# A graph network layer on one core: five groups of edges moved from the dense to the scattered way

## The chip, the core and the metric

The kernel runs on one core of one Trainium2 chip. The metric is the device time of the program in microseconds (us), as the median of several runs. Engines are named as the profile names them: PE is TensorE, ACT ScalarE, DVE VectorE, POOL GpSimd, SP the engine that here only issues transfers.

## The reference, cut to what matters

There are 6250 nodes with 64 features and 200000 edges; the edges are sorted by `dst`, and `src` is random. Each edge's message goes through a small network, the messages are averaged over the edges of the same `src`, and a second network works on the nodes.

```python
h = jnp.maximum(_layernorm(x, axis=-1), 0.0)
row, col = (edge_index[0], edge_index[1])          # row = src, col = dst
msg = jnp.concatenate([h[col], edge_attr], axis=1)
msg = jnp.maximum(msg @ W1a + b1a, 0.0) @ W1b + b1b
summed = jax.ops.segment_sum(msg, row, num_segments=x.shape[0])
counts = jax.ops.segment_sum(jnp.ones((row.shape[0],), msg.dtype), row, num_segments=x.shape[0])
agg = summed / jnp.maximum(counts, 1.0)[:, None]
out = jnp.maximum(jnp.concatenate([h, agg], axis=1) @ W2a + b2a, 0.0) @ W2b + b2b
return x + out
```

## The kernel before

**Tiling.** The edges are cut into 261 groups of 768 (six tiles of 128, `TPG = 6`). For a group, PE first makes the hidden rows: three f32 matmuls of the edge features and six bf16 matmuls that add the rows of the node table (`z`, L1207 and L1212); ACT applies Relu into `r3` (L684, the split). W1b is applied after the averaging, so what is summed over `src` are these hidden rows. There are two ways to sum them, and the constants `DENSE` and `SPARSE` say how many groups go each way.

**The dense way** (140 groups) stays on the chip. PE takes off the bf16 parts to get exact remainders (`take_off`, L1219), routes the rows into ten buckets with one-hot matrices (`route`, 30 matmuls of 196 columns, L1243), ACT copies the buckets out in ten pieces (`keep_routed`, L701). When five groups (`MACRO = 5`, a macro) are in the buckets, PE sums each bucket over its nodes (`sum_nodes`, 150 small matmuls per group, L1257), and DVE makes the one-hots (L937, L952) and adds the sums to `dense` (L959).

**The scattered way** (121 groups) goes through memory. PE adds rows with equal `src` inside a tile (`combine`, 18 matmuls, L1231), ACT copies the result to a slot of `vv` (`keep_rows`, L689), DVE computes which row is to be added where (`pick_first`, L924 and L929), and POOL issues six indirect adding transfers of 128 rows (`scatter`, L524). They go in turn to three tables in memory, `sums0` to `sums2`, and a table takes its next transfer only when its last one has landed. `vv` has four slots (`SR = 4`).

**Order.** All engines walk the same list of cycles, which is what sets the order of all work around the change. A cycle routes one dense group, sums two buckets of the macro before it, and handles no or one scattered group:

```python
for t, n in enumerate(FIRST + BODY + LAST):
    cycle(s, n, Count(t), t < DENSE, t >= MACRO)
```

`n` is the number of scattered groups of cycle `t`. The first five cycles (`FIRST`) have no sums yet, and have `u` matmuls (L1266) in their place; the last five (`LAST`) have sums alone. Between them lie `DENSE - MACRO` = 135 cycles (`BODY`), over which 114 scattered groups are spread as evenly as whole numbers allow: the body cycles without one are numbers 0, 6, 12, 19, 25, 32 and so on, 21 in all. Each engine takes its part of a cycle in its own written order, and waits on semaphores for the others. A scattered group's waits are these:

```python
pool.wait_ge(sidx_ready, done(g.value(1)))             # scatter, POOL
pool.wait_ge(rows_ready, done(g.value(1)))
pool.wait_ge(scattered[t], before.times(16, 16))       # before each of the six
act.wait_ge(comb_ready, done(g.value(1)))              # keep_rows, ACT
act.wait_ge(groups_ended, done(g.value(1 - SR)))
pe.wait_ge(rows_ready, done(g.value(-1)))              # combine, PE
```

So ACT writes group `g` into `vv` only when POOL has issued group `g - 4`; behind that wait stand ACT's other copies of the cycle.

**Ends.** Ahead of the loop the node table is made, and DVE ranks all edges of the dense groups in their buckets with arrays of `DT = (DENSE + 1) * 6` columns (L848 to L889, L873). After the last scatter SP reads the three tables back, POOL adds a bias (L614) and zeroes padding (L618), and a last loop of 13 turns works on the nodes (L1089 to L1129 on DVE, L1318 to L1338 on PE).

Of the kernel before, what the change touches and what calls it, by code (L numbers as in the profile page):

```python
# [47 lines left out]
FIRST_POWER = (127 + 60) * POWER_STEP  # L48
SHIFT = 1.5 * 2.0 ** 23

MACROS = 28
DENSE = MACROS * MACRO
SPARSE = 121
FIRST = (1, 1, 1, 1, 1)
LAST = (1, 0, 1, 0, 0)
EVEN = SPARSE - sum(FIRST) - sum(LAST)
BODY = tuple((t + 1) * EVEN // (DENSE - MACRO) - t * EVEN // (DENSE - MACRO) for t in range(DENSE - MACRO))
DG = DENSE + 1
# [67 lines left out]
def cycles(cycle):  # L126


    s = Count(0)
    for t, n in enumerate(FIRST + BODY + LAST):  # L130
        cycle(s, n, Count(t), t < DENSE, t >= MACRO)
# [3 lines left out]
def gnn_kernel(nc, x, e_t, src_col, dst_col, src_row, dst_row, weights, row_biases, out):  # L135
    f32, i32, i16, bf16 = mybir.dt.float32, mybir.dt.int32, mybir.dt.int16, mybir.dt.bfloat16
    ALU, ACT, AX = mybir.AluOpType, mybir.ActivationFunctionType, mybir.AxisListType
    assert DENSE + SPARSE == GROUPS and GROUPS + 2 <= ALL and DG * TPG <= COLS and 2 * D == P and N_NODES < REAL
    assert N_NODES % NT == 0 and ROWP * ROWG % SIDES == 0 and max(*FIRST, *BODY, *LAST) == 1

    with ExitStack() as ctx:
# [195 lines left out]
        with nc.Block() as block:  # L337

            @block.sync
            def _(sp):  # L340
# [91 lines left out]

                for kind, last in ((S, SPARSE - sum(LAST) + SR + 1), (DN, DENSE + DR + 1)):
                    for s in range(RING[kind]):
# [34 lines left out]
            def _(pool):  # L469
# [83 lines left out]
                with pool.If(fit == 1):  # L553
# [5 lines left out]
                    for t in range(TABLES):  # L559
                        pool.wait_ge(scattered[t], 16 * (1 + len(range(t, SPARSE * TPG, TABLES))))  # L560
                with pool.Else():
# [4 lines left out]
                    def fetch(kind, g):  # L566
                        pool.wait_ge(gidx_ready[kind], done(g.value(1)))
                        pool.sem_inc(pool_past, 1)
                        gather(2 if kind == DN else g.mod(2))
                        if kind == DN:  # L570
                            pool.wait_ge(slots_ready, done(g.value()))
                            pool.dma_start(dsrc, ids[0:1, bass.ds(g.times(GE), GE)].to_broadcast([P, GE])).then_inc(dsrc_in, 16)
# [9 lines left out]
                    def cycle(s, n, t, routes, sums_too):  # L582
                        ended = Count(s.base + min(t.base, DENSE), s.per + t.per, t.turn)
                        for k in range(1, n + 1):
                            if s.per or s.base + k < SPARSE:
                                fetch(S, s.plus(k))
# [40 lines left out]
            def _(act):  # L627
# [48 lines left out]
                def main(fit):  # L676
                    def split(kind, g, r):

                        if r == 0 and not fit:
                            act.wait_ge(zsum_ready[kind], done(g.times(3, 3)))  # L680
                        else:
                            act.wait_ge(z_ready[kind], done(g.times(READS[kind], r + 1)))
                        z = z_ps[kind][:, 0:TPG * D].rearrange("p (t d) -> p t d", d=D)
                        nc.scalar.activation(r3[kind][:, :, PARTS[r]:PARTS[r] + D], z, ACT.Relu).then_inc(split_ready[kind], 1)  # L684

                    def keep_rows(g):
                        act.wait_ge(comb_ready, done(g.value(1)))
                        act.wait_ge(groups_ended, done(g.value(1 - SR)))
                        nc.scalar.activation(vv[:, g.mod(SR), :, :],  # L689
                                             c_ps[g.mod(2)][:, 0:TPG * R].rearrange("p (t w) -> p t w", w=R),  # L690
                                             ACT.Copy).then_inc(rows_ready, 1)
# [28 lines left out]
                    def cycle(s, n, t, routes, sums_too):  # L720
                        if n:
                            keep_rows(s)
                        if n and (s.per or s.base + 1 < SPARSE):
                            split(S, s.plus(1), 0)
# [654 lines left out]
```

## Time and profile before

| | us |
|---|---|
| median of 3 runs | 1632.61 (1630.75 to 1633.25) |
| the profiled execution | 1626.88 |
| its span, first to last instruction | 1625.0 |
| PE busy | 1478.5 (91%) |
| DVE busy | 1416.8 (87%) |
| POOL busy | 1205.2 (74%) |
| ACT busy | 1047.7 (64%) |

The busy times are of one profiled execution, whose own time is 1.88 us over its span and 5.73 us (0.35%) under the median. On POOL only the instruction that issues a transfer counts as busy. It does not count the waits, nor the issue overhead between two of them. Times in the trace are counted from the first instruction.

### The profile page before, as it was taken

What the parts mean: (1) busy time and instruction counts of PE and PEld (TensorE: products, weight loads), DVE (VectorE), ACT (ScalarE), POOL (GpSimd) and SP (SyncE); (2) the same over time, 40 slices, a digit from 0 to 9 for tenths busy, and PEclk for the clock granted to TensorE, in tenths of its full rate; (3) what the DMA queues carried; (4) which work ended last, traced back from release to release, by engine and by line L of the source; (5) the groups of instructions that cost most, each with busy time, mean ns of one, the idle gap of its engine ahead of it and who ended that gap; (6) DMA issues with size and microseconds to landing.
All of it is one profiled execution on the core that took longest, in us unless ns stands there. A gap on an engine that the chain in (4) does not pass through costs nothing.

```text
span 1625.0 us, 77131 instructions
## 1 busy us (share of the span) xinstructions
PE 1478.5 (91%) x31132; PEld 1400.4 (86%) x31132; DVE 1416.8 (87%) x4789; ACT 1047.7 (64%) x2192; POOL 1205.2 (74%) x794
## 2 busy tenths in 40 slices
PE   4378999999999999999999999999999999999946
PEld 3257999999999999999999999999999999899934
DVE  7857988989989899988898988988889989889947
ACT  5167766666666767666666667766666767666503
POOL 5166777788778788777787788787777878777771
PEclk9689999999999999999999999999999999999977
DMA  5666776767767677666677766776767767667651
GB/s 174 239 118 99 122 106 107 122 107 108 120 105 118 111 113 119 105 115 109 105 123 106 118 108 109 122 109 107 115 110 118 113 105 125 104 113 109 95 118 58
DMA packets 279402, 187.16 MB, mean 115 GB/s; under 512 B 190543, under 2 KB 275404, under 8 KB 278281
## 3 DMA queue, kind: packets, MB, share of 16 engines
q1 hardware_dynamic: 174070, 152.93, 39.5%
q0 software_dynamic: 104976, 29.30, 27.7%
q8 instruction: 246, 4.03, 1.0%
q14 instruction: 110, 0.90, 0.2%
HBM read 147.94 MB, written 34.17 MB: 112 GB/s over the span
## 4 chain that ended last, share of the span: by engine, by line
PE 73%; ACT 11%; issue 5%; DMA 5%; DVE 3%; POOL 2%; DVEq 0%; SPq 0%; POOLq 0%; ACTq 0%
PE l_ps L1257 31%; PE l_ps L1243 22%; PE z_ps L1207 8%; ACT area L701 7%; PE z_ps L1219 5%; PE c_ps L1231 5%; DMA sums<-vv,sidx 3%; ACT r_d L684 3%; PE z_ps L1212 2%; POOL sums L524 1%; DMA area<-sums 1%; DMA xs<-in_x 1%; DVE rank L873 1%; ACT r_s L684 0%; DVE area L857 0%
## 5 line engine op out<-in xcount | busy, mean ns | idle before, releaser
L524 POOL DMA_INDIRECT sums<-vv,sidx x726 | 1157.5, 1594 | 359.6 <-issue 169.7
L1257 PE MATMUL l_ps<-area 128*128 128x64 bf16 (+1 forms) x21000 | 793.0, 193 | 1.0 <-issue 0.4
L701 ACT ACTIVATE area<-l_ps 64x392 bf16<-64x392 f32 x1400 | 688.1, 491 | 127.4 <-PE l_ps L1243 97.1
L1257 PEld LDWEIGHTS l_ps<-area 128*128 128x128 bf16 x21000 | 746.0, 98 | 22.8 <-issue 1.9
L1243 PE MATMUL l_ps<-r_d,oh 128*128 128x196 bf16 x4200 | 483.6, 250 | 16.0 <-issue 8.3
L952 DVE TENSOR_SCALAR area<-iota,local 128x640 bf16<-128x640 int16 x1400 | 475.4, 404 | 4.9
L1243 PEld LDWEIGHTS l_ps<-r_d,oh 128*128 128x128 bf16 x4200 | 334.5, 96 | 26.9 <-ACT area L701 12.2
L684 ACT ACTIVATE r_d<-z_ps 128x384 f32<-128x384 f32 x423 | 207.8, 491 | 196.5 <-PE z_ps L1219 182.2
L937 DVE TENSOR_SCALAR oh<-iota,rank 128x640 bf16<-128x640 int16 x846 | 281.7, 401 | 0.0
L959 DVE TENSOR_TENSOR dense<-l_ps,dense 128x325 f32<-128x325 f32 x280 | 137.8, 492 | 115.2 <-PE l_ps L1257 110.0
L917 DVE TENSOR_TENSOR r_s<-r_s 128x384 f32<-128x384 f32 x242 | 134.3, 555 | 4.1
L1219 PE MATMUL z_ps<-r_d,minus_b 128*128 128x384 bf16 x282 | 96.1, 341 | 44.5 <-ACT r_d L684 28.4
L906 DVE TENSOR_SCALAR same<-ids_s,srcf 128x128 bf16<-128x128 int16 x726 | 131.2, 269 | 0.0
L689 ACT ACTIVATE vv<-c_ps 128x396 f32<-128x396 f32 x121 | 60.5, 500 | 94.2 <-PE c_ps L1231 93.7
L1207 PE MATMUL z_ps<-wts,et_d 128*128 128x128 f32 x846 | 121.1, 280 | 0.0
L1207 PE MATMUL z_ps<-wts,et_s 128*128 128x128 f32 x726 | 112.5, 292 | 2.4 <-issue 2.4
L1207 PEld LDWEIGHTS z_ps<-wts,et_d 128*128 128x128 f32 x846 | 105.8, 192 | 0.0
L684 ACT ACTIVATE r_s<-z_ps 128x384 f32<-128x384 f32 x121 | 59.1, 488 | 71.0 <-PE z_ps L1212 69.1
L1231 PE MATMUL c_ps<-r_s,same 128*128 128x64 bf16 (+1 forms) x2178 | 93.1, 193 | 2.0 <-issue 1.8
L1207 PEld LDWEIGHTS z_ps<-wts,et_s 128*128 128x128 f32 x726 | 92.3, 195 | 2.6 <-issue 2.5
L899 DVE TENSOR_SCALAR hots_d<-ids_d,basew 128x384 bf16<-128x384 int16 x284 | 84.3, 337 | 0.0
L1231 PEld LDWEIGHTS c_ps<-r_s,same 128*128 128x128 bf16 x2178 | 78.1, 97 | 6.4 <-issue 2.4
(133 smaller groups left out, 737.0 us busy)
## 6 DMA issues: line engine op xcount, KB each, us to landing
ids_s<-ids SPq DMA_DIRECT2D x248, 192.0 KB
et_d<-in_e_t SPq DMA_DIRECT2D x143, 192.0 KB
ids_d<-ids SPq DMA_DIRECT2D x143, 192.0 KB
et_s<-in_e_t SPq DMA_DIRECT2D x124, 192.0 KB
sums<-vv,sidx POOLq DMA_INDIRECT x726
sums<-dense POOLq DMA_DIRECT2D x3, 1657.5 KB
wp_d<-p_table SPq DMA_DIRECT2D x286, 15.8 KB
wp_s<-p_table SPq DMA_DIRECT2D x248, 15.8 KB
```

Source lines behind the costliest of these rows:

```text
L524: nc.gpsimd.indirect_dma_start(out=sums[t][:, :], out_offset=bass.IndirectOffsetOnAxis(ap=index, axis=0), in_=rows, in_offset=None, comput ...
L684: nc.scalar.activation(r3[kind][:, :, PARTS[r]:PARTS[r] + D], z, ACT.Relu).then_inc(split_ready[kind], 1)
L701: ins = nc.scalar.activation(routed[on, t.div(MACRO).mod(2), first:second + 1:second - first, t.mod(MACRO), :], bank[on, :, :], ACT.Copy)
L917: nc.vector.tensor_tensor(r3[S][:, :, PARTS[r + 1]:PARTS[r + 1] + D], r3[S][:, :, at:at + D], halves(S)[:, :, at:at + D], ALU.subtract).th ...
L937: ins = nc.vector.tensor_scalar(oh1[:, k, :], iota[:], pos[:, bass.ds(t.value(k * DG), 1)], None, ALU.is_equal)
L952: nc.vector.tensor_scalar(oh2[:, g, :], iota[:], local[:, n.mod(2), g:g + 1], None, ALU.is_equal).then_inc(nodes_ready, 1)
L959: nc.vector.tensor_tensor(part, l2_ps[h][:, 0:BW], part, ALU.add).then_inc(summed, 1)
L1207: nc.tensor.matmul(z_ps[kind][:, j * P:(j + 1) * P], et[kind][:, slot, j * P:(j + 1) * P], wts[:, C_W1A_BOT:C_W1A_BOT + P], start=j == 0, ...
L1219: nc.tensor.matmul(z_ps[kind][:, 0:TPG * D], minus_b[:], halves(kind)[:, :, PARTS[r]:PARTS[r] + D], start=False, stop=True, skip_group_che ...
L1231: t = nc.tensor.matmul(c_ps[b][:, k * R:k * R + n], same[:, b, k, :], halves(S)[:, k, PARTS[r]:PARTS[r] + n], start=r == 0, stop=r == 2)
L1243: ins = nc.tensor.matmul(l1_ps[f % 2][:, i * RW:(i + 1) * RW], oh1[:, k, block * P:(block + 1) * P], halves(DN)[:, k, :], start=k == side ...
L1257: ins = nc.tensor.matmul(l2_ps[h][:, u * W:u * W + w], oh2[:, g, u * P:(u + 1) * P], rows[:, PARTS[r]:PARTS[r] + w], start=g % MACRO == 0 ...
```

## The change

Three constants change. One macro less goes the dense way: 27 macros, 135 groups. The scattered groups become 126. The last cycle gets a scattered group, so there are five in the first five cycles, 118 over the 130 of the body and three in the last five. The number of groups stays 261, and the order within a cycle stays as it is. The body has twelve cycles without a scattered group, numbers 0, 10, 21, 32, 43 and so on.

```diff
-MACROS = 28
+MACROS = 27
 DENSE = MACROS * MACRO
-SPARSE = 121
+SPARSE = 126
 FIRST = (1, 1, 1, 1, 1)
-LAST = (1, 0, 1, 0, 0)
+LAST = (1, 0, 1, 0, 1)
```

In the body on ACT, the first place where the two orders differ is the end of cycle 11, body number 6. In these rows `vv` is the copy of a scattered group, `r_s` the Relu of the next one, `area` the ten bucket copies of a dense group and `r_d` its three splits. Before:

```order
L689 ACTIVATE vv<-c_ps 128x396
L684 ACTIVATE r_s<-z_ps 128x6x64
L701 ACTIVATE area<-l_ps 64x2x196 x10
L684 ACTIVATE r_d<-z_ps 128x6x64 x3
L701 ACTIVATE area<-l_ps 64x2x196 x10
L684 ACTIVATE r_d<-z_ps 128x6x64 x3
L689 ACTIVATE vv<-c_ps 128x396
```

And now, in the same cycles:

```order
L689 ACTIVATE vv<-c_ps 128x396
L684 ACTIVATE r_s<-z_ps 128x6x64
L701 ACTIVATE area<-l_ps 64x2x196 x10
L684 ACTIVATE r_d<-z_ps 128x6x64 x3
L689 ACTIVATE vv<-c_ps 128x396
L684 ACTIVATE r_s<-z_ps 128x6x64
L701 ACTIVATE area<-l_ps 64x2x196 x10
```

The cycle without `vv` and `r_s` is gone from here; the next one comes four cycles later, and such cycles are eleven apart instead of six or seven.

At the end of the main loop on ACT, the rows begin with the last cycle of the body. Before:

```order
L689 ACTIVATE vv<-c_ps 128x396
L684 ACTIVATE r_s<-z_ps 128x6x64
L701 ACTIVATE area<-l_ps 64x2x196 x10
L684 ACTIVATE r_d<-z_ps 128x6x64 x3
L689 ACTIVATE vv<-c_ps 128x396
L684 ACTIVATE r_s<-z_ps 128x6x64
L689 ACTIVATE vv<-c_ps 128x396
```

And now:

```order
L689 ACTIVATE vv<-c_ps 128x396
L684 ACTIVATE r_s<-z_ps 128x6x64
L701 ACTIVATE area<-l_ps 64x2x196 x10
L684 ACTIVATE r_d<-z_ps 128x6x64 x3
L689 ACTIVATE vv<-c_ps 128x396
L684 ACTIVATE r_s<-z_ps 128x6x64
L689 ACTIVATE vv<-c_ps 128x396
L684 ACTIVATE r_s<-z_ps 128x6x64
L689 ACTIVATE vv<-c_ps 128x396
```

Two scattered groups followed the body's last, and now three do.

## Rows read from the trace of the kernel before

**Rows 1.** The page: span, busy time, share, instructions; then groups of part 5.

```profile
span 1625.0 us, 77131 instructions
PE 1478.5 (91%) x31132; PEld 1400.4 (86%) x31132; DVE 1416.8 (87%) x4789; ACT 1047.7 (64%) x2192; POOL 1205.2 (74%) x794
...
L524 POOL DMA_INDIRECT sums<-vv,sidx x726 | 1157.5, 1594 | 359.6 <-issue 169.7
```

**Rows 2.** Busy time of each engine in four stretches, clock, DMA share, GB/s.

```profile
core 0: us, PE busy (x) PEld busy (x) DVE busy (x) ACT busy (x) POOL busy (x), PEclk, DMA share, GB/s
141.80:1532.50 1390.70, 1344.94 (x29638) 1294.81 (x29639) 1257.49 (x4340) 958.86 (x1985) 1086.90 (x682) 1.00 0.71 112
1532.50:1559.40 26.90, 25.75 (x775) 24.21 (x772) 21.64 (x66) 0.99 (x2) 22.63 (x15) 1.00 0.38 29
1559.40:1565.80 6.40, 0.00 (x0) 0.00 (x0) 0.50 (x1) 0.00 (x0) 5.45 (x4) 0.76 0.31 19
1565.80:1625.00 59.20, 28.94 (x130) 20.12 (x130) 37.56 (x104) 14.60 (x39) 17.91 (x17) 0.67 0.34 113
```

**Rows 3.** The scatters of L524 alone, in two stretches: POOL busy and count.

```profile
154.60:1508.70 1354.10, 1062.60 (x666) 1.00 0.71 112
1508.70:1565.80 57.10, 47.55 (x30) 0.97 0.51 64
```

**Rows 4.** What POOL waited for, 154.6 to 1508.7: us, times, longest.

```profile
POOL sums L524 <- issue: 156.6, 481, 2.4
POOL sums L524 <- DMA sums<-vv,sidx: 104.4, 173, 2.4
POOL sums L524 <- DVE sidx L929: 36.4, 12, 6.9
```

**Rows 5.** Instructions of POOL in order of time: start, us, idle before.

```profile
88.63 1.68 POOL L524 DMA_INDIRECT sums<-vv,sidx  x1 [40.05 <-DVE sidx L929]
...
154.67 1.55 POOL L524 DMA_INDIRECT sums<-vv,sidx  x1 [6.94 <-DVE sidx L929]
...
1472.41 1.56 POOL L524 DMA_INDIRECT sums<-vv,sidx  x1 [2.85 <-DVE sidx L929]
...
1508.78 1.55 POOL L524 DMA_INDIRECT sums<-vv,sidx  x1 [1.05 <-DMA sums<-vv,sidx]
...
1564.22 1.55 POOL L524 DMA_INDIRECT sums<-vv,sidx  x1 [0.30 <-issue]
1570.47 7.18 POOL L614 TENSOR_TENSOR xs<-xs,rowb 128x3328 f32<-128x3328 f32 x1 [4.70 <-issue]
```

**Rows 6.** Instructions of PE in order of time, at cycle borders.

```profile
141.86 0.70 PE L1243 MATMUL l_ps<-r_d,oh 128*128 128x196 bf16 x6 [0.57 <-ACT ht L717]
...
181.94 0.72 PE L1231 MATMUL c_ps<-r_s,same 128*128 128x66 bf16 x18
...
192.51 0.71 PE L1231 MATMUL c_ps<-r_s,same 128*128 128x66 bf16 x18
...
211.97 0.71 PE L1231 MATMUL c_ps<-r_s,same 128*128 128x66 bf16 x18
...
1532.57 10.31 PE L1257 MATMUL l_ps<-area 128*128 128x65 bf16 x300
```

**Rows 7.** What ACT's copy to `vv` waited for, whole span.

```profile
ACT vv L689 <- PE c_ps L1231: 93.7, 79, 10.2
```

**Rows 8.** The chain that ended last, near its end: start, us.

```profile
1564.22 3.28 DMA sums<-vv,sidx
1567.65 2.66 issue
1570.57 0.35 SPq L445
...
1603.14 0.41 PE l_ps L1318 x2
...
1614.29 0.66 PE l_ps L1318 x2
```

**Rows 9.** Groups by shape: busy, mean ns; ranking of the dense edges.

```profile
L873 DVE COPY_PREDICATED rank<-area,l_ps 128x423 f32<-128x423 uint16 x20 | 11.4, 622 | 1.1 <-PE l_ps L1183 0.2
L857 DVE TENSOR_SCALAR area<-area 128x846 bf16<-128x846 f32 x10 | 5.2, 591 | 0.0
```

**Rows 10.** Busy time in the second half of the first cycles.

```profile
120.00:142.00 22.00, 15.76 (x167) 13.12 (x166) 12.88 (x48) 16.91 (x35) 17.38 (x11) 0.95 0.69 111
```

## The prediction

> **What bounds the kernel now.** I read the busy times first, and they point to PE: 91% of the span, and 1344.94 of 1390.70 us in the body of the main loop, from the first routing matmul at 141.86 to the last cycle's end at 1532.57 [rows 1, 2, 6]. By the same rows POOL looks free, with 74% of the span. A change that takes work from PE and gives it to POOL then looks like a clear gain. The second view to read is POOL's waits, because its busy time leaves out what stands between two scatters. From 154.67, where the first group of the body starts, to 1508.78 POOL issued 666 scatters, 111 groups, in 1354.1 us, 12.20 us each [rows 3, 5]. In that time it waited for DVE's indices, that is for work, 36.4 us, and 6.94 of them lie before the first scatter of the stretch [rows 4, 5]. So it was short of work for only 29.5 us. The rest of its idle time is the overhead of issue and waits for an earlier scatter to land, and these come with every group. **A scattered group costs POOL (1354.1 - 29.5) / 111 = 11.93 us**, of which 1062.60 / 111 = 9.57 are busy [rows 3]. POOL is thus occupied for 98% of the stretch (1324.6 / 1354.1). The third view is the end: PE has nothing after 1559.4, while POOL issues until 1565.77, its last transfer lands at 1567.5, and only then does the final stage begin [rows 2, 5, 8]. So two engines bound the kernel, nearly equally, and POOL is the one that ends last.
>
> **PE's side of a cycle.** Matmuls of `combine` start at 181.94 and 192.51, one cycle with a scattered group apart: 10.57 us. The next starts at 211.97, after one with and one without: 19.46, so a cycle without costs 19.46 - 10.57 = 8.9 [rows 6]. I take 9.0, since over the body 1390.7 = 114 x T + 21 x 9.0 then gives T = 10.54, which fits the 10.57. With these two costs the 29.5 us come out again: between two empty cycles (6.43 cycles apart, 5.43 groups) PE takes 5.43 x 10.54 + 9.0 = 66.2 us and POOL 5.43 x 11.93 = 64.8, so POOL idles 1.4 us in each of 21 stretches, 29 us in all. That agreement is why I trust 11.93 as a cost that does not depend on how short of work POOL is.
>
> **What the change takes from PE.** The body becomes 118 cycles of 10.54 and 12 of 9.0, 1351.7 us, or 39.0 less. On average PE then offers a scattered group every 1351.7 / 118 = 11.46 us. Of the work in the cycles nothing else changes; DVE (1257.49 of 1390.70 busy in the body, [rows 2]) and ACT lose with the five dense groups more than five scattered ones give them.
>
> **What it gives to POOL.** POOL needs 11.93 us where PE offers one each 11.46. Now an empty cycle comes after 9.83 groups, for which PE takes 9.83 x 10.54 + 9.0 = 112.6 us and POOL 117.3. POOL falls 4.7 us further behind in each of these twelve stretches and is never short of work after its first body group; the 29.5 us vanish, and that is all the slack there is. Its own waits before that point stay: the first scatter comes at 88.63, and body number 0 is empty in both kernels, so the 6.94 us stay [rows 5]. When POOL is three groups behind (3 x 11.93 = 36 us, after some eight of the twelve stretches), the four slots of `vv` are full: ACT waits for POOL before L689, behind it stand ACT's bucket copies, and PE waits for those. That stall costs nothing more, since POOL has three groups in hand then; it only takes back the time PE had won. Before, no such wait shows but one: the longest of ACT before L689 is 10.2 us, and all 93.7 us are put down to PE [rows 7].
>
> **The sum.** From 154.67 POOL had 116 groups to do and has 121 now. In the last stretch, where few loads run beside it, five groups took 57.1 us, 11.42 each, at a DMA share of 0.51 against 0.71 [rows 3]. I count seven groups of that kind now: POOL is up to four behind when the body ends, and three follow. So 114 x 11.93 + 7 x 11.42 = 1360.0 + 79.9 = 1439.9 us, against 1565.8 - 154.67 = 1411.1 before: **+28.8 us**. The ranking ahead of the loop works on 816 columns instead of 846, 3.5% of some 20 us of DVE work on that chain (11.4 and 5.2 are its two largest groups, [rows 9]): -0.7. The final stage of 59.2 us waits for POOL alone and stays [rows 2, 8]. PE will have been idle longer when it begins, but it begins at the lower of its two levels already: the granted clock over the stage is 0.67 [rows 2], and its transposes take 0.66 us a pair against 0.41 at the higher one [rows 8]. I bound a shift of the clock's rise at 2 us either way and take 0. The third group in the last five cycles adds 0.7 us of `combine` to PE [rows 6] and one copy to ACT; both hide under POOL's backlog, and without that they would cost 1 to 2 us. All together +28.1. On the profiled execution that is 1626.9 + 28.1 = 1655.0 with a span of 1653; on the median of the runs shown, 5.7 above it, **1632.6 + 28 = 1661**.
>
> **How sure the 11.93 is.** Everything hangs on it: 0.1 us is 11 us in the time. Below, the nearest row is the 11.42 of the last stretch; above, the three groups from 1472.41 to 1508.78 took 12.12 each [rows 3, 5]. Each bound is an end, over 114 groups: -58 us and +22 us. I keep the middle value because the body's loads per time hardly change. A dense group's features and ids come at each 10.4 us instead of each 10.3, and the scattered groups' loads come a little closer in the time before the slots are full.
>
> The SBUF page of the Trainium skill (SBUF — State Buffer, section "SBUF: two separate sides") says that some DVE operations lock a port pair that GpSimd needs, and that GpSimd then cannot write the descriptors of its transfers. By that rule a less busy DVE would make scatters shorter. The trace leaves little for it: a scatter took 1.595 us on average in the body (1062.60 / 666) and 1.585 in the last stretch [rows 3], so even if all of this were gained, it would be 6 x 0.01 x 114 = 7 us, and the change leaves DVE nearly as busy.
>
> **The rivals.** (1) **POOL keeps up and PE is the bound.** If landings become quicker, because fewer dense loads compete, and a group falls to 11.46 us or less, POOL follows PE. Then the body ends at 141.9 + 1351.7 = 1493.6, POOL issues its last 33.2 us later as now (1565.77 - 1532.57) and 11.4 more for the third group: 1538.2. That is 27.6 us earlier, a time of 1605. For it: 11.42 was seen, at a DMA share of 0.51. Against it: a group needs 9.57 us of issue alone, the overhead is at each scatter, and the share in the body will stay near 0.7, since loads follow cycles. The DMA page of the skill (DMA: Bandwidth & Descriptors, section "SWDGE vs HWDGE vs iDMA") says that each DMA engine takes turns between the queues of the two kinds of transfer, which would make a landing depend on the loads beside it; the two rows agree in direction. (2) **A cheaper scatter, but not enough.** Between 11.6 and 11.75 us a group the gain and the loss meet: no change lies at 11.93 - 28 / 114 = 11.68. This decides from 0.25 us less waiting, half of what a group waits now beyond the overhead of about 0.3 us at each of six scatters (11.93 - 9.57 - 1.8 = 0.56). (3) **Scatters collide more.** With ten scattered groups in a row instead of five or six, 12.12 us may be the rule: +22 more, 1683. (4) **The stall at full slots costs PE its clock.** With ACT waiting, PE could fall to its lower level and cycles grow beyond POOL's pace, so that POOL starves again. In the first cycles PE was busy 15.76 of 22 us, less than it would be here, and was still granted 0.95 [rows 10]. So I take it as small: 10 us or so on top, 1671, within the range. That the change does not do what it says is not in question: the constants alone set the cycles.
>
> **How the numbers follow.** POOL-bound near 11.93, 1645 to 1677: 0.77. More collisions or a clock loss beyond that: 0.09. The middle case, about 1632 to 1645: 0.07, of which 0.03 within 0.2% and 0.04 above it. PE-bound or near it, under 1629: 0.07. Two tenths of a percent, 3.3 us, is about what a measurement of this kernel can tell from no change. Faster is 0.07, same 0.03, slower 0.77 + 0.09 + 0.04 = 0.90. The range of 1640 to 1679 leaves out the PE-bound case, a part of the middle one and the far end of the collisions, some 0.16.
>
> **What would show it.** In the profile after: scatters x756; POOL waiting for DVE's indices under 55 us in the whole span, of which 40.05, 6.94 and a little lie before 155; 11.9 us a group in the body; the last scatter at about 1594; PE's matmuls ending some 40 us or more before it, where it was 6.4; ACT waiting several times, for over 1 us, before L689 late in the body; PE busy about 40 us less. It would be wrong if a group cost under 11.7 us, and then POOL's waits for landings would be the row that moved; or if POOL still waited for indices every eleven cycles.

## The result and the profile after

| | before | after |
|---|---|---|
| median of 6 runs each, us | 1632.89 (1626.44 to 1633.79) | 1640.05 (1638.41 to 1647.67) |
| ratio, 95% interval | | 1.0077 [1.0053, 1.01] |
| the profiled execution, its span | 1626.88, 1625.0 | 1639.26, 1637.5 |

The changed kernel is 7.2 us slower by the medians, and 12.4 us by the two profiled executions. Forecast were 28 us. The direction held and the size did not.

The page of the changed kernel answers [rows 1]: span, busy time, and the group of the scatters.

```profile
span 1637.5 us, 75449 instructions
PE 1449.8 (89%) x30312; PEld 1371.8 (84%) x30312; DVE 1399.0 (85%) x4739; ACT 1017.2 (62%) x2137; POOL 1253.6 (77%) x824
...
L524 POOL DMA_INDIRECT sums<-vv,sidx x756 | 1206.0, 1595 | 325.2 <-issue 179.3 <-DMA sums<-vv,sidx 97.4 <-DVE sidx L929 47.9
```

PE lost 28.7 us of busy time and the kernel got slower. The scatters are 756 as they must be, and one still takes 1595 ns of POOL (1594 before). What shrank is the idle time before them: 325.2 us for 756, where 359.6 stood before 726.

The stretches of [rows 3] again, the scatters of L524 alone, with the borders moved to the start of the last six groups: 115 groups of the body, then those six. Columns: window, length, POOL busy and count, clock, DMA share, GB/s.

```profile
153.60:1511.00 1357.40, 1101.42 (x690) 0.99 0.70 113
1511.00:1580.00 69.00, 57.15 (x36) 0.86 0.42 46
```

And instructions of POOL, the counterpart of [rows 5]: start, us, idle before.

```profile
153.69 1.56 POOL L524 DMA_INDIRECT sums<-vv,sidx  x1 [8.38 <-DVE sidx L929]
...
1578.03 1.55 POOL L524 DMA_INDIRECT sums<-vv,sidx  x1 [0.31 <-issue]
1584.05 7.18 POOL L614 TENSOR_TENSOR xs<-xs,rowb 128x3328 f32<-128x3328 f32 x1 [4.47 <-issue]
```

A group took 1357.4 / 115 = 11.80 us in the body. The last six took 68.6 / 6 = 11.43 each, and all 121 took 1579.58 - 153.69 = 1425.9 us, 11.78 each. The forecast had 11.93 in the body.

The waits over the whole span, the counterpart of [rows 4, 7]: us in total, times, longest.

```profile
POOL sums L524 <- DMA sums<-vv,sidx: 97.4, 186, 2.3
POOL sums L524 <- DVE sidx L929: 47.9, 2, 39.5
...
ACT vv L689 <- PE c_ps L1231: 77.3, 61, 10.4
ACT vv L689 <- POOLq L539: 65.6, 24, 10.9
...
PE l_ps L1243 <- ACT area L701: 34.9, 35, 2.6
```

POOL waited for DVE's indices twice, 39.5 and 8.4 us, both before 153.7, and never again. POOL is now the only bound of the body. The backlog shows in the last two rows. ACT waited 24 times for POOL to free a slot of `vv`, a wait that the kernel before does not show; behind it stood the bucket copies, and PE waited 34.9 us for those, where it was 5.4 before.

The end of the span, the counterpart of [rows 2].

```profile
1560.00:1579.60 19.60, 0.00 (x0) 0.00 (x0) 0.00 (x0) 0.00 (x0) 16.53 (x11) 0.59 0.31 19
1579.60:1637.50 57.90, 29.31 (x130) 20.08 (x130) 37.27 (x104) 14.61 (x39) 18.13 (x17) 0.65 0.35 115
```

In the first window POOL works alone: PE, DVE and ACT have nothing. The final stage takes 57.9 us, 1.3 less than before.

### The profile page after: what moved, and what is told of

Its sections match the earlier page's. It is cut to its first block and busy times, and to the rows that moved or that the text cites. A ratio compares the mean times of both kernels' runs of the same rounds, so it can differ in the third digit from the quotient of the medians.

```text
span 1637.5 us, 75449 instructions
## 1 busy us (share of the span) xinstructions
PE 1449.8 (89%) x30312; PEld 1371.8 (84%) x30312; DVE 1399.0 (85%) x4739; ACT 1017.2 (62%) x2137; POOL 1253.6 (77%) x824
## 5 line engine op out<-in xcount | busy, mean ns | idle before, releaser
L524 POOL DMA_INDIRECT sums<-vv,sidx x756 | 1206.0, 1595 | 325.2 <-issue 179.3
L1257 PE MATMUL l_ps<-area 128*128 128x64 bf16 (+1 forms) x20250 | 770.0, 194 | 0.5 <-DVE area L952 0.3
L1257 PEld LDWEIGHTS l_ps<-area 128*128 128x128 bf16 x20250 | 724.1, 98 | 22.0 <-issue 0.7
L701 ACT ACTIVATE area<-l_ps 64x392 bf16<-64x392 f32 x1350 | 663.0, 491 | 116.7 <-PE l_ps L1243 88.1
L1243 PE MATMUL l_ps<-r_d,oh 128*128 128x196 bf16 x4050 | 470.8, 251 | 51.0 <-ACT area L701 34.9
L952 DVE TENSOR_SCALAR area<-iota,local 128x640 bf16<-128x640 int16 x1350 | 457.8, 403 | 4.8
L1243 PEld LDWEIGHTS l_ps<-r_d,oh 128*128 128x128 bf16 x4050 | 325.1, 97 | 63.7 <-ACT area L701 42.9
L684 ACT ACTIVATE r_d<-z_ps 128x384 f32<-128x384 f32 x408 | 200.5, 491 | 193.5 <-PE z_ps L1219 183.2
L937 DVE TENSOR_SCALAR oh<-iota,rank 128x640 bf16<-128x640 int16 x816 | 274.0, 403 | 0.0
L689 ACT ACTIVATE vv<-c_ps 128x396 f32<-128x396 f32 x126 | 63.1, 501 | 162.5 <-PE c_ps L1231 77.3
L1231 PE MATMUL c_ps<-r_s,same 128*128 128x66 bf16 x2268 | 96.9, 193 | 2.0 <-issue 1.8
L684 ACT ACTIVATE r_s<-z_ps 128x384 f32<-128x384 f32 x126 | 61.4, 487 | 58.6 <-PE z_ps L1212 57.9
```

The costliest lines, as they stand in the source:

```text
L524: nc.gpsimd.indirect_dma_start(out=sums[t][:, :], out_offset=bass.IndirectOffsetOnAxis(ap=index, axis=0), in_=rows, in_offset=None, comput ...
L701: ins = nc.scalar.activation(routed[on, t.div(MACRO).mod(2), first:second + 1:second - first, t.mod(MACRO), :], bank[on, :, :], ACT.Copy)
L937: ins = nc.vector.tensor_scalar(oh1[:, k, :], iota[:], pos[:, bass.ds(t.value(k * DG), 1)], None, ALU.is_equal)
L952: nc.vector.tensor_scalar(oh2[:, g, :], iota[:], local[:, n.mod(2), g:g + 1], None, ALU.is_equal).then_inc(nodes_ready, 1)
L1231: t = nc.tensor.matmul(c_ps[b][:, k * R:k * R + n], same[:, b, k, :], halves(S)[:, k, PARTS[r]:PARTS[r] + n], start=r == 0, stop=r == 2)
L1243: ins = nc.tensor.matmul(l1_ps[f % 2][:, i * RW:(i + 1) * RW], oh1[:, k, block * P:(block + 1) * P], halves(DN)[:, k, :], start=k == side ...
```

## Experiments

Two things had to be explained: why the loss was 7 us and not 28, and whether the loss comes from POOL at all. **Theory**: the time follows the slower of two paces, PE's per cycle and POOL's per scattered group, and the change moves work from the one to the other. **Rivals**: the price is POOL's alone whatever PE does; it is the stall at full slots; or it is ACT, which stands between the two.

The experiments ran in five sets, on four chips: `e1` to `e4`, `e5` to `e8`, `e9` to `e12`, `e13` and `e14` (on the chip of `e5` to `e8` again), and `e15` to `e18`. The kernel before took 1619.6, 1616.2, 1616.4, 1617.1 and 1628.1 us in the five sets, and 1632.9 us in the recorded comparison, whose chip is not known. Each ratio below is against the kernel before in the same set. That difference turned out to matter, and has a part of its own.

### Both kernels again

`e5` and `e9` are the kernel before, `e6` and `e10` the changed one, on two chips.

> The kernel before, unchanged, for a profile on the same chip as the next three. With 145 dense groups and with four tables PE's cycles took 9.89 us with a scattered group and 8.76 without, all alike, where the first profile of the kernel before had 10.48 and 9.24 on average. Theory A, PE's own pace differs between chips: here the cycles are 9.9 to 10.1 us wherever POOL does not stop them, the 114 groups are then offered each 11.5 us, POOL at 12.0 us cannot follow, and the kernel before is bound by POOL too, with many waits of ACT for POOL before L689. Theory B, the longer cycles belong to this split of the groups with three tables: they are 10.4 us or more here as well, with hardly a wait of ACT for POOL.

> The changed kernel, unchanged, on the same chip. Theory A, if the kernel before is bound by POOL here: the change adds five groups at POOL's full price with no slack to take up, 5 x 12.0 = 60 us less a few for shortages, so a ratio of about 1.03 instead of 1.008. Theory B, if PE still sets the pace of the kernel before: 7 to 15 us more, a ratio of 1.004 to 1.009.

> The kernel before, unchanged, once more, since the chip may be another. Two kinds of profile of it have been seen: PE's cycles of 9.89 us where POOL does not stop them, with POOL never short of work in the body (time 1615), and cycles of 10.48 us on average with POOL short of work for 29.5 us (time 1633). Theory A, the kind belongs to the chip: this profile is of the one or the other, and the ratio of the next run follows it. Theory B, it belongs to the single execution: this profile may be of another kind than the ratio of the next run asks for.

> The changed kernel, unchanged, beside it. Theory A: where the kernel before shows cycles of 9.89 us and no shortage, a ratio of 1.03; where it shows 10.4 us or more and a shortage of about 30 us, a ratio of 1.007. Theory B: no such link.

| | us | ratio to before on the same chip |
|---|---|---|
| e5, before | 1614.82 | 0.9996 [0.9972, 1.002] |
| e6, after | 1669.44 | 1.0343 [1.0292, 1.0393] |
| e9, before | 1616.24 | 0.9989 [0.9971, 1.0007] |
| e10, after | 1665.54 | 1.0287 [1.0257, 1.0317] |

Here the change costs 49 to 55 us, seven times the recorded 7. What ACT and POOL waited for in `e5`, the kernel before:

```profile
POOL sums L524 <- DMA sums<-vv,sidx: 118.4, 182, 2.4
ACT vv L689 <- POOLq L539: 113.7, 40, 10.3
POOL sums L524 <- DVE sidx L929: 48.2, 5, 40.2
```

The kernel before is here where the changed kernel was in the recorded trace: ACT waits 40 times for POOL, and of POOL's 48.2 us of waiting for work all but 1.2 us lie before its first body group. From there on it needs 12.04 us a group (116 groups from 153.49 to 1550.43), and `e6` 12.03. There is no slack to use up, so five groups more cost 5 x 12.03 = 60 us of POOL. The spans of the two profiled pairs differ by 59.6 and 57.4 us, the medians by 55 and 49.

### More and fewer scattered groups

```diff
-MACROS = 27
-SPARSE = 126
+MACROS = 26
+SPARSE = 131
```

> One macro less still: 26 macros, 130 dense and 131 scattered groups (123 of them in the 125 body cycles). Theory A, POOL sets the pace of the changed kernel, and a scattered group costs it 11.8 us: five more groups add 5 x 11.8 = 59 us to the changed kernel's 1640, so 1699, and ACT waits for POOL before L689 in most cycles. Theory B, the changed kernel is slower for another reason (its last five cycles, or stalls that are lost to all engines) and PE still sets the pace of the body: PE has another 39 us less to do, and the time stays at or under 1640.

Measured: 1727.19 us, 1.0666 [1.0626, 1.0706]. That is 107.6 us over the kernel before in the same set, for ten groups more; the first five cost 53 us in the set of `e6`, so the next five cost about 54, for 60 of POOL. The stall grows to 336.0 us before L689 and PE waits 180.9 us for ACT, and the time still grows by no more than POOL's groups. The loss is POOL's groups, one after the other.

```diff
-MACROS = 28
-SPARSE = 121
+MACROS = 29
+SPARSE = 116
```

> One macro more than before: 29 macros, 145 dense and 116 scattered groups (109 in the 140 body cycles). Theory A, the kernel before is bound by PE in its body and POOL only just keeps up: the body is 109 x 10.54 + 31 x 9.0 = 1428 us, 37 more than before, and POOL waits for indices in it for about 37 + 5 x 11.9 = 95 us more; the time is 1633 + 37 = 1670. Theory B, POOL sets the pace of the kernel before too: 5 groups less on it give 1633 - 59 = 1574, or at least under 1633.

Measured: 1588.57 us, 0.9812 [0.978, 0.9843], 31 us faster than the kernel before. This decides for theory B of the expectation: on this chip POOL sets the pace of the kernel before as well, where the prediction had the two engines nearly equal. A step the other way gains, but 31 us and not 60, because PE becomes the bound and POOL is short of work for 36 us in the body. Three equal stretches of `e2`, with the busy time of PE, PEld, DVE, ACT and POOL:

```profile
160.00:560.00 400.00, 398.37 (x9017) 390.45 (x9015) 379.95 (x1304) 297.42 (x606) 307.63 (x193) 1.00 0.70 115
560.00:960.00 400.00, 398.19 (x9014) 390.00 (x9012) 379.98 (x1303) 296.17 (x603) 311.26 (x195) 1.00 0.70 114
960.00:1360.00 400.00, 398.37 (x9016) 390.45 (x9014) 378.35 (x1294) 297.26 (x605) 308.06 (x194) 1.00 0.70 114
```

The same stretch of the kernel before as recorded:

```profile
160.00:560.00 400.00, 387.88 (x8545) 373.34 (x8542) 363.05 (x1252) 276.33 (x572) 312.64 (x196) 1.00 0.71 112
```

In `e2` PE is hardly ever idle: 9017 matmuls in 400 us against 8545. This is PE's own pace, and from its instructions a cycle with a scattered group takes 9.89 us and one without 8.77, on average, with hardly any spread. The forecast had read 10.54 and 9.0 in the recorded trace. Those were not the pace that PE has when nothing holds it up, although PE looked busy 97% of that stretch. By its own pace PE's body in the kernel before needs 114 x 9.89 + 21 x 8.77 = 1312 us, far less than the 116 x 12.04 = 1397 that POOL needs; that is why `e5` has no slack.

### The wait for landings

A scattered group costs POOL 9.57 us of issuing and 1.8 of overhead; the rest is waiting until the table's last transfer has landed. A fourth table in memory gives each landing more time: the scatters of the body go in turn to four. (The branch for inputs that the dense way can't hold isn't run here, and stays at three.)

```diff
-TABLES = 3
+TABLES = 4
+GT = 3
...
-        AREA = MACRO * BUCKETS * RW + BUCKETS * LOCAL // 2 + GE // 2
+        AREA = max(TABLES * NTP * W, MACRO * BUCKETS * RW + BUCKETS * LOCAL // 2 + GE // 2)
...
+                    nc.gpsimd.tensor_tensor(tab[2][:, part], tab[2][:, part], tab[3][:, part], ALU.add).then_inc(pool_half, 1)
+                    pool.wait_ge(pool_half, done(m + 1))
```

> The changed kernel with a fourth table in memory for the scatters, so that a table gets each fourth transfer instead of each third; the fourth table is zeroed, read back and added at the end like the others. Theory A, what a scattered group costs POOL beyond issue and overhead is waiting for the table's last landing: this wait nearly vanishes, a group costs about 6 x (1.595 + 0.30) = 11.4 us, and PE becomes the bound at 11.46 us a group: 1640 - 115 x 0.34 = 1601, with 3 to 6 us more for zeroing and reading a fourth table 1604 to 1607. Theory B, the landings are slow because the transfer engines are loaded, and the wait only moves to another place (the issue itself, or the loads of SP): a group still costs 11.7 us or more, and the time is 1640 to 1646.

> The kernel before with a fourth table. Theory A, PE sets the pace of its body: POOL's shorter groups only lengthen its waits for indices (from 29 to about 80 us), the body stays 1390 us, and the time is 1633 plus 0 to 6 us for the fourth table, minus at most 4 us of backlog at the end. Theory B, POOL's landings hold back the body of the kernel before too: it gets faster by more than 10 us.

Measured: the changed kernel with four tables 1599.6 us, 0.9874 [0.9842, 0.9906]; the kernel before with four tables 1553.23 us, 0.959 [0.9559, 0.9621]. **The second is the best version found**: 66 us faster than the kernel before on the same chip, and faster than the changed one. What its POOL waited for:

```profile
POOL sums L525 <- DVE sidx L933: 55.4, 8, 39.4
POOL sums L525 <- DMA sums<-vv,sidx: 41.5, 135, 0.5
```

The expectation of `e4` had PE as the bound and no gain, and was wrong as that of `e2` was. The longest wait for a landing is 0.5 us and no more 2.4 (in `e3` it is 1.4, for 2.8 in `e6`). A group takes 11.43 to 11.46 us (shortage left out) for 12.02 to 12.06 with three tables. So about 0.6 us of a group are waits for landings that a fourth table takes away, and 0.6 x 121 = 73 us is what this is worth. Of these, 5 us go to the final stage, which has a table more to read and to add (63.1 us from the last scatter to the end, for 58.0 in `e5`), and 7 us to shortage of work in the body, for PE is busy 398.9 of 400 us there; 66 were measured. The price of the change is nearly the same with four tables: 1599.6 - 1553.2 = 46 us.

The other way to shorten a landing is to take loads away. `e8` is the changed kernel without the loads of the dense groups' ids after the first two groups (their one-hots are then made from old ids, so this part of the input is left out).

```diff
-                    load_ids(kind, nxt)
+                    if kind == S:
+                        load_ids(kind, nxt)
...
-                    dve.wait_ge(ids_in[kind][slot], g.div(SR).times(32, 32) if kind == S else g.div(DR).times(16, 16))
+                    dve.wait_ge(ids_in[kind][slot], g.div(SR).times(32, 32) if kind == S else 16)
```

> The changed kernel without the loads of the dense groups' dst numbers (192 KB a group) after the first two groups; the old numbers are used, which changes no work on any engine. Theory A, a scatter lands late because of the loads that run beside it: with a tenth of the transfers gone the excess of POOL's gaps over 0.30 us falls from 0.4 to 0.7 us a group to under 0.3, and the time by 20 us or more. Theory B, the landing time is the table's own and does not depend on the loads: POOL's gaps and the time stay within 5 us.

Measured: 1656.33 us, 1.0257 [1.0209, 1.0305], 13 us under `e6`; a group takes 11.93 us for 12.03, x 121 = 12 us. That lies between the two theories of the expectation, which had 20 us or more and 5 or less. The loads beside do lengthen a landing, and 0.1 us a group is the size of it. The DMA page of the Trainium skill (DMA: Bandwidth & Descriptors, "SWDGE vs HWDGE vs iDMA") says that each DMA engine takes turns between the two kinds of queue; the run agrees in direction. The DMA share from 160 to 1560 us fell only from 0.69 to 0.62, a tenth, so this bounds what a small change of the loads can do, not what all of them cost.

### The stall at full slots

POOL announces an ended group `LAG` groups late.

```diff
-LAG = 2
+LAG = 1
```

> The changed kernel with LAG 1 instead of 2: ACT may write a group to its slot of vv one group of POOL earlier, so that POOL can be some 25 us behind instead of some 14. Theory A, POOL sets the pace and is never short of work: the time stays within 3 us of the changed kernel's, ACT's waits for POOL shrink in the first third and come back later. Theory B, the stalls of ACT and PE at the full slots cost time at the end: it is faster by 10 us or more.

Measured: 1669.01 us, 1.0343 [1.0295, 1.0391], against `e6` 1669.44 beside it. ACT may run one group further ahead, and the time doesn't move: the stall costs nothing, as forecast. It does touch TensorE's clock, as rival 4 of the prediction had it: the granted clock was 0.99 in the body of the recorded changed kernel (1.00 before) and 0.97 in that of `e6`. PE was not the bound there, so this cost nothing either. Nor did a group cost POOL more or less with the larger backlog (12.05 us for 12.03).

### ACT slower

Is it ACT that sets the cycles? `e11` and `e12` add one copy of 384 columns (about 0.5 us) behind each `keep_rows`, to before and after; `e13` and `e14` add two in every routing cycle.

```diff
+                        if routes:
+                            for at in (t.base % 2, 2 + t.base % 2):
+                                nc.scalar.activation(stage[:, 512 * at:512 * at + 384], iota[:, 0:384], ACT.Copy)
```

> The kernel before with one more copy of 384 numbers on ACT (about 0.5 us) behind each keep_rows, ahead of the copies of the cycle; its result is used nowhere. It makes PE's cycles with a scattered group some 0.5 us longer where ACT's chain sets them, as the recorded profile shows them. Theory A, the price of the change depends on how much slack POOL has: the cycles become about 10.4 us, POOL gets short of work in the body for some 10 to 40 us, and the time rises by 5 to 20 us over the kernel before on a chip with short cycles. Theory B, POOL sets the pace with or without it: the time stays within 3 us.

> The changed kernel with the same copy on ACT. Theory A: POOL is never short of work in the body, and the time stays within 5 us of the changed kernel's; the difference between the two slowed kernels is 35 to 50 us, less than the 53 us between the two kernels as they are. Theory B: the difference stays 53 us or more.

> The kernel before with two more copies of 384 numbers on ACT (some 1 us together) in every cycle that routes, ahead of the split of the next group; their results are used nowhere. Theory A, the kernel before sits where PE's pace and POOL's cross, and the sign of the change follows from which is slower: cycles become about 10.9 us with and 9.7 without a scattered group, the body 114 x 10.9 + 21 x 9.7 = 1446 us against POOL's 114 x 12.05 = 1374, so about 70 us more than the kernel before, 1685, and POOL short of work in the body for some 70 us. Theory B, the time hangs on POOL's transfers alone: it stays under 1625, as with the one copy.

> The changed kernel with the same two copies. Theory A: PE needs 118 x 10.9 + 12 x 9.7 = 1403 us and POOL 118 x 12.05 = 1422, so POOL still sets the pace: about 1670, as without the copies, and 10 to 20 us less than the kernel before with the copies, so the change gains where PE is slowed. Theory B: the difference between the two kernels stays what it is, 53 us against the change. If in the slowed pair a scattered group's price of 12.05 us also falls towards 11.8, the lower price in the recorded profiles would come with the slower cycles.

| | us | ratio to before on the same chip |
|---|---|---|
| e11, before with one copy | 1615.85 | 0.9992 [0.9968, 1.0016] |
| e12, after with one copy | 1672.85 | 1.0322 [1.0278, 1.0366] |
| e13, before with two | 1617.91 | 1.0001 [0.9979, 1.0023] |
| e14, after with two | 1671.06 | 1.0321 [1.027, 1.0371] |

One more us of ACT in each cycle changes nothing, before or after, where the copies were put. Cycles that nothing stalled still took 9.89 us in `e13`, where 10.9 had been expected. So ACT has that much room at that place, and the change's price is still 53 to 57 us. But as the copies did not slow the cycles, these four runs do not test the theory of two paces.

### TensorE slower

The last pair of pairs slows PE alone, with 10 or 18 matmuls more in each routing cycle, whose results nobody uses.

```diff
+                    for _ in range(10 if routes else 0):
+                        nc.tensor.matmul(l1_ps[0][:, 392:512], ident_b[:], ones_b[:, 0:120], start=True, stop=True, skip_group_check=True)
```

> The kernel before with 10 matmuls more (128x120, results unused) in every routing cycle, so that TensorE alone is slower by an estimated 0.55 us a cycle (some 55 ns each). Balance of two paces: cycles of about 10.4 us with a scattered group and 9.3 without, TensorE's routing needs 114 x 10.44 + 21 x 9.31 = 1386 us, more than GpSimd's 1372; time some 1630 to 1640 us, GpSimd short of work for 15 to 40 us. Rival (the price lies in GpSimd alone): time stays at 1615 to 1618, since TensorE had room.

> The changed kernel with the same 10 matmuls a cycle. Balance of two paces: 118 x 10.44 + 12 x 9.31 = 1344 us of TensorE under GpSimd's 1420, so GpSimd still sets the end: 1666 to 1670 us, and the difference to the kernel before with the same matmuls shrinks from 53 to about 35 us. Rival: the difference stays at 50 to 53 us. If a scattered group costs GpSimd less when TensorE is slower (11.8 for 12.05 us, as in the recorded pair), the time is 1640 instead.

> The kernel before with 18 matmuls more in every routing cycle (an estimated 1.0 us a cycle). Balance of two paces: cycles of 10.89 and 9.76 us, TensorE's routing needs 114 x 10.89 + 21 x 9.76 = 1446 us, 75 more than GpSimd's 1372: 1680 to 1695 us. Rival: 1615 to 1630.

> The changed kernel with the same 18 matmuls a cycle. Balance of two paces: 118 x 10.89 + 12 x 9.76 = 1402 us of TensorE, still under GpSimd's 1420: 1668 to 1675 us, so that the change is now faster by 10 to 25 us than the kernel before with the same matmuls. Rival: slower by 50 us as without them.

| extra matmuls a cycle | before, us | after, us | after minus before |
|---|---|---|---|
| 10 | 1682.33 (1679.39 to 1685.65) | 1662.02 (1658.15 to 1669.99) | -20.3 |
| 18 | 1731.01 (1729.83 to 1731.62) | 1702.69 (1698.91 to 1708.39) | -28.3 |

**The sign turned round.** With PE slower, the changed kernel is the faster one, and the ranges of the runs don't touch. The theory of two paces stands, and that the price is POOL's alone falls: ten small matmuls on PE made the kernel before 54 us slower than it was on the same chip (1628.1 us). The changed kernel without extra matmuls was not run on this chip, so from what value its difference fell to -20 us is not shown; it was +7 in the recorded pair and +49 to +55 on two other chips. The expectations missed: `e15` by 42 to 52 us; `e16` came 4 us under its range, but the difference was to be about +35 and is -20; `e17` by 36 us or more and `e18` by 28 or more. They were worked out from cycles of 9.89 us, and this chip's are longer (next part): in the traces cycles take 10.96 us with a scattered group and 9.50 without in `e15`, where 10.4 and 9.3 were expected. What POOL waited for DVE's indices, in `e15`, `e16`, `e17` and `e18` in this order; 50 to 57 us of each lie ahead of the body's second scatter:

```profile
POOL sums L524 <- DVE sidx L929: 144.2, 24, 40.3
```

```profile
POOL sums L524 <- DVE sidx L929: 50.7, 4, 39.5
```

```profile
POOL sums L524 <- DVE sidx L929: 192.3, 28, 39.9
```

```profile
POOL sums L524 <- DVE sidx L929: 110.1, 19, 39.4
```

In `e15` POOL starves and PE is the bound; in `e16` POOL is, as after the recorded change; with 18 matmuls PE is in both (POOL is short of work for 53 us in the body of `e18`), and then the change gains because it leaves PE less to do.

## Two lengths of a cycle, and what differs in the trace

PE's instructions last equally long in all traces, and yet the cycles do not. The recorded pair and the chip of `e15` to `e18` show long ones (10.48 and 9.24 us in the recorded kernel before), the chips of the other runs short ones (9.89 and 8.77). The place where they part is the hand-over from PE to ACT within a dense group. Two rows each of the timeline, `e2` first: start, us, what; PE's `take_off` and ACT's next split.

```profile
706.89 0.33 PE L1219 MATMUL z_ps<-r_d,minus_b 128*128 128x384 bf16 x1
...
707.26 0.49 ACT L684 ACTIVATE r_d<-z_ps 128x384 f32<-128x384 f32 x1 [0.59 <-PE z_ps L1219]
```

And the recorded kernel before:

```profile
704.94 0.33 PE L1219 MATMUL z_ps<-r_d,minus_b 128*128 128x384 bf16 x1
...
706.15 0.49 ACT L684 ACTIVATE r_d<-z_ps 128x384 f32<-128x384 f32 x1 [1.43 <-PE z_ps L1219]
```

ACT was idle and starts 0.37 us after the start of the matmul in the first, 1.21 us after it in the second. From 200 to 1400 us I compared all such places where ACT was idle:

| trace | places | median, us | over 0.6 us | longest, us |
|---|---|---|---|---|
| recorded, before | 234 | 0.38 | 64 | 1.25 |
| recorded, after | 225 | 0.39 | 65 | 1.22 |
| e15 | 224 | 0.38 | 67 | 1.25 |
| e2 | 248 | 0.38 | 0 | 0.39 |
| e5 | 236 | 0.38 | 0 | 0.39 |
| e10 | 218 | 0.37 | 0 | 0.39 |

In some traces ACT now and then begins up to 0.9 us late, in others never. The split of the example is the third, which no `take_off` waits for; most of the late ones (50 of 64) are of this kind. But the bucket copies ahead of the splits begin late as well. Where ACT was idle before one that waits for routing, it began 0.28 us after the start of the last routing matmul in `e2`, `e4` and `e5` (median; 0.40 at most), and 0.65 us after it in the recorded kernel before (1.3 at most). This pushes the first split back, and PE's first `take_off` waits for it. Three rows of the recorded kernel before: a late copy, the first split, the first `take_off`.

```profile
702.28 1.00 ACT L701 ACTIVATE area<-l_ps 64x392 bf16<-64x392 f32 x2 [0.57 <-PE l_ps L1243]
703.30 0.49 ACT L684 ACTIVATE r_d<-z_ps 128x384 f32<-128x384 f32 x1
703.85 0.34 PE L1219 MATMUL z_ps<-r_d,minus_b 128*128 128x384 bf16 x1 [0.40 <-issue]
```

PE's waits there, in the recorded kernel before, in `e15`, and in `e5`:

```profile
PE z_ps L1219 <- ACT r_d L684: 28.4, 76, 1.0
```

```profile
PE z_ps L1219 <- ACT r_d L684: 34.5, 83, 1.0
```

```profile
PE z_ps L1219 <- ACT r_d L684: 9.0, 12, 1.0
```

Taken from one start to the next, PE's steps from the sums into the two `take_off`s come to 0.52 us in an average cycle with a scattered group of the recorded kernel before, and to 0.07 in `e2`: 0.44 of the 0.59 us by which the cycle is longer. That locates the difference; that the late starts are its cause is argued from these rows and not shown by a run. `e13` had ACT busier by 1 us a cycle without effect, but its copies lay elsewhere, ahead of the scattered group's split. That the kind of trace belongs to the chip is likely and not more: two sets on one chip gave 1616.2 and 1617.1 us for the kernel before, but no trace of it was taken on the chip of `e15` to `e18`. Why ACT begins late in one and not in the other the traces don't tell.

## Why the prediction was right in direction and wrong in size

**Right**: POOL is the bound, although it has the lower busy share; the 29.5 us of shortage are all used up (POOL never waits for work after 153.7); scatters x756; POOL's waits for indices, 47.9 us, under the 55 that were named; ACT waits before L689; the final stage follows POOL alone; the stall at full slots costs nothing (`e7`, `e1`). Right in direction only: PE busy 28.7 us less, for about 40; and PE's matmuls end 18.6 us before the last scatter starts (1559.5 against 1578.0), where over 40 was forecast with the last scatter at 1594.

**The step that failed is the price of a scattered group.** The mechanism held, and this term of the sum was too large. The sum took 11.93 us from the kernel before as "a cost that does not depend on how short of work POOL is". The recorded trace after shows 11.80 in the body, without any shortage. The stretch that was to take 1439.9 us took 1425.9: -14.0 us. The final stage gave 1.3 more and the start of the body 0.3. That makes 12.4 us in the profiled pair where 28.1 were forecast. The other 5 us of the miss, between 12.4 and the 7.2 of the medians, are no mechanism: the profiled execution of before was 6.0 us under its median and the one of after 0.8.

The price was trusted for a reason that could not test it. The 29.5 us of shortage came out twice, once from POOL's waits and once from PE's cycles; but both divide the same stretch of the same body (1354.1 us for 111 groups by POOL's scatters, 1390.7 for 114 by PE's cycles, 12.20 us each), so they agree at any price.

Where the 0.13 us went is visible, why is not. A scatter's own time stayed; the waits for landings fell from 111.9 us for 726 scatters to 97.4 for 756. The prediction had put this case at 0.07 ("a cheaper scatter, but not enough", 11.6 to 11.75 us), and said rightly which row would move. Fewer loads beside are not the cause: 0.1 us needed a tenth of the DMA share gone (`e8`), and that of the body went from 0.71 to 0.70. Nor is it how far POOL is behind (`e7`). All traces with three tables and all loads together say a little more. This is the price from the body's first scatter to the end of the last, with the waits for indices taken out, in us a group:

| pair | before | after |
|---|---|---|
| recorded | 11.91 | 11.78 |
| e15, e16 | 11.87 | 11.96 |
| e17, e18 | 11.82 | 11.86 |
| e5, e6 | 12.03 | 12.02 |
| e9, e10 | 12.10 | 12.07 |

The other seven such traces (`e1`, `e2`, `e7`, `e11` to `e14`) lie at 12.02 to 12.13. So the price is lower, before and after, where the cycles are of the long kind, and the change by itself does not lower it: it moved by -0.13 in the recorded pair, by +0.09 and +0.04 in the next two, and by -0.01 and -0.03 in the last two. Between traces it varies by some 0.1 us, which is 12 us in the time, nearly as much as the sum missed. What makes it vary stays open.

**A second error did no harm in the recorded pair, and would have elsewhere.** The prediction took cycles of 10.54 us for PE's own pace. Where `e5` to `e14` ran PE's pace is 9.89, the shortage is 1.2 us instead of 29.4, and the change costs 49 to 55 us. The forecast of 28 lies between the two measured values. Side by side, by PE's cycle with a scattered group where POOL doesn't stall it:

| PE's cycle in the kernel before, us | 9.89 | 10.48 | 10.96 (e15) | 11.31 (e17) |
|---|---|---|---|---|
| POOL short of work in its body, us | 1 | 29 | 92 | 137 |
| after minus before, us | +49 to +55 | +7 | -20 | -28 |

The 9.89 of the first column is from `e2` and `e4`, its other values are from `e5`, `e6`, `e9` and `e10`; the second column is the recorded pair. The more POOL is short of work, the more of the five groups it can take without cost, and the more the relief of PE is worth.

**A wrong detail** is that the four slots of `vv` are full only when POOL is three groups behind (36 us). POOL counts a group as ended late, by `LAG = 2`, which the semaphore's first value carries:

```python
pool.sem_inc(groups_ended, START - LAG)
```

So ACT may write group `g` only when POOL has issued `g - 2`, and not `g - 4` as the description of the kernel has it too. The first stalls came early in the body, at 329 us, not after eight stretches, and PE could not get as far ahead as forecast. Of the sum only the count of cheap groups at the end hung on it: seven were counted, six seen, 0.5 us.

The Trainium skill (SBUF — State Buffer, "SBUF: two separate sides") says that GpSimd cannot write descriptors while DVE runs an operation that holds their shared port pair. That a less busy DVE would shorten scatters, as the prediction worked out from it, the recorded pair does not show: DVE went from 87% to 85% of the span and a scatter from 1594 to 1595 ns. Over all traces there is a slight lean that way: 1588 ns in `e17`, where DVE is busy 84% of the time from 160 to 1360 us, and 1605 ns in `e4`, where it is 96%. These kernels differ in more than that, and it is 0.1 us a group at most.

## What to carry to other kernels

An engine that issues transfers is bound by busy time, overhead and landing waits together; divide the stretch by the groups and take out only the time in which it had no work. Give such a price the spread that several traces show before a sum over a hundred groups rests on it. When a change shifts work between two engines of nearly equal pace, its sign is the difference of the paces, so find each engine's own pace with a run in which it alone is the bound (here a kernel with five scattered groups fewer), and test the sign by slowing one of them. Before shifting work, look for what the busy engine waits for: one more table was worth 66 us, nine times what moving groups had cost in the recorded pair.

## What the runs showed of the hardware that was not expected

The same program took 1615 to 1633 us in different sets, with equal durations of its instructions; what differs is that in some traces ACT begins up to 0.9 us late at 64 of 234 places, and in others at none. An indirect adding transfer of 128 rows costs POOL 1.59 to 1.61 us (means of all traces) and 0.30 us of overhead behind it, and three tables in turn (3 x 1.89 = 5.7 us between two transfers to the same one) are not quite enough to hide its landing, while four are but for waits of 0.5 us (`e4`) and 1.4 us (`e3`) at the longest.
